# Row gathers of the last layer in bursts of 12, 8 and 12 instead of four bursts of 8

## The chip, the cores and the metric

The kernel runs on one core of a Trainium2 chip. The metric is the device time of one execution in microseconds (us), from runs of the whole program; lower is better. The rows and sums further down come from one profiled execution of the kernel before.

## What is computed

Four message-passing layers on a graph of 8192 nodes (32 features each) and 262144 edges sorted by destination. Each layer adds its result to x and normalises the rows:

```python
edge_index = jnp.stack([src, dst])
x = _layernorm(x + _L0_gnn_ref(x, L0_gnn_weight, src, dst, edge_type_64), axis=-1)
x = _layernorm(x + _L1_gnn_ref(x, edge_index, edge_weight), axis=-1)
x = _layernorm(x + _L2_gnn_ref(x, edge_index), axis=-1)
x = _layernorm(x + _L3_gnn_ref(x, edge_index, edge_attr_4, edge_attr_32, W1, b1, W2, b2, si_w0, si_w1), axis=-1)
```

The change touches the last layer, `_L3_gnn_ref`. For each edge a small network turns 32 edge features into 256 weights, and the message is made of these weights, of the source node's row (8 scalars s and 8 vectors v) and of 4 numbers sh of the edge:

```python
h = jax.nn.relu(edge_feat @ W1 + b1)
w = (h @ W2 + b2).reshape(e, 4, MUL, MUL)
s_e = s[src]
v_e = v[src]
m0 = ALPHA * (einsum('ei,eio->eo', s_e * sh0[:, None], w_000) + C110 * einsum('eim,em,eio->eo', v_e, sh1, w_110))
m1 = ALPHA * (einsum('ei,em,eio->eom', s_e, sh1, w_011) + einsum('eim,eio->eom', v_e * sh0[:, None, None], w_101))
out0 = jax.ops.segment_sum(m0, dst, num_segments=n)
out1 = jax.ops.segment_sum(m1.reshape(e, MUL * 3), dst, num_segments=n)
```

`s[src]` and `v[src]` are a gather of one row of 32 floats per edge.

## The kernel before

The edges are cut into 128 chunks of 2048. A chunk is 16 tiles of 128 edges, and 4 tiles are a group, so a chunk has 4 groups. The last layer holds four chunks at a time in the slots s = 0 to 3 of the buffer `gathered`; chunk c uses slot c mod 4. A pass of a loop over `it` handles four chunks, 32 passes (ROUNDS) in all.

For each chunk of the last layer the engines do this:

- **SP** (`stage(3)`, from L505): waits until the slot is free (`slot_freed`), then loads the 2048 source indices (`idx`, L512), the edge features (L515) and sh (L518).
- **POOL** (`gather_chunk`, L619 to L629): waits for the indices (L622) and issues 16 indirect DMAs (L626). Each fetches 128 rows of x by 128 indices, and tells of its landing on the semaphore of its group, `group_in[s][j // GROUP]`. Before some of the 16 it calls `pace(j)`, which for the last layer is `rests_3` (L668 to L674): where j is in RESTS_3, `rows_landed` (L662 to L666) makes POOL wait until the last group issued so far has landed. The first four chunks are gathered without any pacing (L694), the other 124 in the loop at L696.
- **PE** (`chunk3`): transposes the next chunk's edge features (L1285), makes its hidden units (L1296), multiplies out the weights of its groups (L1305), and sums the messages of the chunk before into destination windows with one-hot matrices (L1074).
- **ACT** (`chunk3`): copies and relu of the edge network (L904, L910), `scale_rows` of each group, which scales gathered rows by sh0 (L920, waits for `group_in`), and the one-hot matrices (L776, L789).
- **DVE** (`messages`, L1929 to L1980): 11 operations for each group; the first, `cprod` (L1940), waits for `group_in` as well and stands once per group. Then `add_chunk` (L1657 to L1669) and `release`, which frees the slot for SP.

So POOL can be up to four chunks ahead of DVE, and it is DVE's release that lets it into a slot. At the end of the layer ACT and DVE normalise most blocks beside the last chunks (L943 to L973, L2007 to L2021) and the last 8 blocks after the last chunk.

What sets the rests before the change:

```python
RESTS_3 = (0, 8)
...
if j in RESTS_3:
    rows_landed(s, j)
```

Of the kernel before, what the change touches and what calls it, by code (L numbers as in the profile page):

```python
# [9 lines left out]
SLOTS = 4  # L10
# [22 lines left out]
AHEAD = 12  # L33
MARKS_0 = [{8}, {2, 27}, {20}, {2, 27}, {20}, {13}, {0, 21}, {8, 30}]
MARKS_LATE = 2
RESTS_3 = (0, 8)
LEAD_0, LEAD_LATE = 6, 6
AHEAD_HI = 2
AHEAD_PARTS = 5
# [31 lines left out]
def build(nc, x, src, dst, edge_attr_32, edge_attr_4, edge_type_64, edge_weight, L0_gnn_weight,  # L71
# [15 lines left out]
    SET_LIST = [(n, m) for n in range(len(PARTS)) for m in range(2 if n < AHEAD_PARTS else 0, CHUNKS // WIDE)]  # L87
    SETS = len(SET_LIST)
    LOAD_SETS = [i for i, (n, _) in enumerate(SET_LIST) for _ in range(PARTS[n][1] // 4)]
    AHEAD_STEPS, AHEAD_STD = 6 * (ROUNDS - AHEAD), 2 * (ROUNDS - AHEAD)  # L90
    assert EARLY == TRIO * ROUNDS and LATE % SLOTS == 0 and WIDE * STRIP_D == SUPER * P
# [3 lines left out]
    with ExitStack() as ctx:  # L95
# [145 lines left out]
        rest = arena[:, 4096 * LOADS + 512:4096 * LOADS + 512 + BLOCKS * F].rearrange("p (b f) -> p b f", f=F)  # L241
# [183 lines left out]
        def is_dense(eng):  # L425

            eng.wait_ge(dense_known, 1)
            return numbers_at(eng, dense_ok[0:1, 0:1], 0, 1)[0]

        def is_regular(eng):  # L430

            eng.wait_ge(regular_known, 1)
            return numbers_at(eng, regular_ok[0:1, 0:1], 0, 1)[0]
# [27 lines left out]
        def looped(eng, first, end):  # L461

            return nc.Fori(first, end, engines=bass.OrderedEngineSet([eng.engine]), hint_back_edge=True)
# [136 lines left out]
        @block.gpsimd  # L600
        def _(pool):
            pool.iota(iota_i[:, :], [[1, P]], base=1, channel_multiplier=0).then_inc(iota_done, 1)
            pool.iota(part_i[:, :], [[1, 1]], base=0, channel_multiplier=1).then_inc(iota_done, 1)
            pool.iota(iota4_i.rearrange("p (c j) -> p c j", j=LANES), [[1, P], [0, LANES]], base=1,
                      channel_multiplier=0).then_inc(iota_done, 1)
            pool.iota(dst_of[:, :], [[P, BLOCKS + 2]], base=0, channel_multiplier=1).then_inc(iota_done, 1)

            pool.wait_ge(first_ready, 1)
            pool.wait_ge(records_out, 32)
            for b in range(BLOCKS):  # L610
                pool.indirect_dma_start(
                    csr[:, b, :, :].rearrange("p k w -> p (k w)"), None, records,
                    bass.IndirectOffsetOnAxis(ap=first_at[:, b:b + 1], axis=0)).then_inc(csr_in, 16)
            for k in range(4):
                pool.wait_ge(table_stored[k], 16 * (BLOCKS // TABLE_GROUP))
            due = [pool.alloc_register(f"idx_due_{s}") for s in range(SLOTS)]
            for s in range(SLOTS):
                pool.reg_mov(due[s], 16)
            def gather_chunk(l, s, pace=None):  # L619

                pool.wait_ge(idx_in[s], pool.snap(due[s]))
                pool.reg_add(due[s], due[s], 16)  # L622
                for j in range(TILES):
                    if pace is not None:
                        pace(j)
                    pool.indirect_dma_start(  # L626
                        gathered[:, s, j, :], None, rows[l],
                        bass.IndirectOffsetOnAxis(ap=idx[:, s, j:j + 1], axis=0),
                    ).then_inc(group_in[s][j // GROUP] if l == 3 else rows_in[l][s], 16)  # L629

            def gather(l):

                if l >= 1:
                    pool.wait_ge(rows_out[l - 1], 16)
                with looped(pool, 0, ROUNDS):
                    for s in range(SLOTS):
                        gather_chunk(l, s)

            regular = is_regular(pool)  # L640
            with pool.If(regular):
                mark = pool.alloc_register("mark_due")
                by_round = sum(len(marks) for marks in MARKS_0)

                def mark_passed():

                    pool.wait_ge(pe_mark, pool.snap(mark))
                    pool.reg_add(mark, mark, 1)

                def marks_0(j):  # L650

                    if j % (TRIO * TILES // by_round) == 0:
                        mark_passed()

                def marks_late(j):

                    if j % (TILES // MARKS_LATE) == 0:
                        mark_passed()

                landed = {(s, rest): pool.alloc_register(f"landed_{s}_{rest}") for s in range(SLOTS) for rest in RESTS_3}  # L660

                def rows_landed(s, rest):  # L662

                    last = (s - (rest == 0)) % SLOTS, (rest - 1) % TILES
                    pool.wait_ge(group_in[last[0]][last[1] // GROUP], pool.snap(landed[s, rest]))
                    pool.reg_add(landed[s, rest], landed[s, rest], 16 * GROUP)  # L666

                def rests_3(s):  # L668

                    def pace(j):  # L670

                        if j in RESTS_3:
                            rows_landed(s, j)
                    return pace  # L674

                pool.reg_mov(mark, by_round + 1 - LEAD_0)
                for s in range(TRIO):
                    gather_chunk(0, s)
                with looped(pool, 1, ROUNDS):
                    for s in range(TRIO):  # L680
                        gather_chunk(0, s, marks_0)
                pool.reg_mov(mark, ROUNDS * by_round + 1 - LEAD_LATE)
                with looped(pool, 0, LATE // SLOTS):
                    for s in range(SLOTS):
                        gather_chunk(0, s, marks_late)
                dense = is_dense(pool)
                with pool.If(dense < 1):
                    gather(1)
                    gather(2)
                for s in range(SLOTS):  # L690
                    for rest in RESTS_3:
                        pool.reg_mov(landed[s, rest], 16 * GROUP * (1 + (s > 0 or rest > 0)))
                pool.wait_ge(rows_out[2], 16)
                for s in range(SLOTS):  # L694
                    gather_chunk(3, s)
                with looped(pool, 1, ROUNDS):  # L696
                    for s in range(SLOTS):
                        gather_chunk(3, s, rests_3(s))
            with pool.Else():
                for l in range(4):  # L700
                    gather(l)
# [1369 lines left out]
```

## Time and profile before

| | us |
|---|---|
| median of 3 runs | 7251.59 |
| lowest and highest run | 7243.55, 7280.37 |
| profiled execution: its time | 7251.99 |
| profiled execution: span from the first to the last instruction | 7250.2 |
| PE busy in that span | 5598.4 (77%) |
| DVE busy | 4279.9 (59%) |
| POOL busy | 3945.7 (54%) |
| ACT busy | 2999.4 (41%) |

The last layer's gathers begin at 4127.8 us of the span and its messages at 4226.2 us, so it fills about the last 3000 us. In the rows of the profile, times are us from the start of the span, "x" counts instructions, and a bracket at the end of a timeline row gives how long the engine sat idle before the instruction and what ended that. "L626" is the line that issues the gathers. A busy POOL is here a POOL that writes the descriptors of a gather; the transfer itself runs on the DMA engines after that.

### The profile page before, as it was taken

The page shows a single profiled execution, that of the slowest core. Times are in us where ns is not written, and L with a number is a line of the kernel's source. Part 1 is how long each engine was busy: PE and PEld are TensorE (multiplying, and loading weights), DVE is VectorE, ACT ScalarE, POOL GpSimd, SP SyncE. Part 2 cuts the span into 40 slices and gives each one's busy share as a digit, 9 for nine tenths or more (in the row PEclk, how much of TensorE's full clock was granted, in tenths as well). Part 3 has the DMA queues.
Part 4 walks back from the last instruction along what each step waited for, and adds up shares of the span by engine and source line. Part 5 has one row for each costly group of instructions (what it writes and reads, how often), then busy time and mean ns, then how long its engine had stood idle before and what let it go on. Part 6 is the DMA issues. An engine that isn't in the chain of part 4 may idle for free.

```text
span 7250.2 us, 118009 instructions
## 1 busy us (share of the span) xinstructions
PE 5598.4 (77%) x38929; PEld 4300.2 (59%) x38930; DVE 4279.9 (59%) x8297; ACT 2999.4 (41%) x7294; POOL 3945.7 (54%) x4168
## 2 busy tenths in 40 slices
PE   7377777777777777666667668888888888888888
PEld 3177777676776766533333346666666666666666
DVE  4166656655556565311111058877887887888788
ACT  4244444444444444200000045555555555555556
POOL 1445555555555555555550146666666666666665
PEclk7587777777777778666667767777777777777777
DMA  9433333444444444687879601111111111111111
GB/s 318 145 150 145 141 136 130 165 162 149 171 151 163 150 162 163 211 283 269 277 242 296 199 15 25 24 23 24 24 24 23 24 24 23 24 24 24 23 25 24
DMA packets 596643, 865.44 MB, mean 119 GB/s; under 512 B 170833, under 2 KB 418706, under 8 KB 579474
## 3 DMA queue, kind: packets, MB, share of 16 engines
q1 hardware_dynamic: 363858, 385.79, 16.8%
q10 hardware_dynamic: 99520, 406.06, 14.2%
q0 software_dynamic: 133120, 71.57, 5.3%
q8 instruction: 102, 1.67, 0.1%
q14 instruction: 43, 0.35, 0.0%
HBM read 455.19 MB, written 406.85 MB: 119 GB/s over the span
## 4 chain that ended last, share of the span: by engine, by line
PE 37%; issue 24%; POOL 23%; another core or an unknown queue 5%; ACT 5%; DMA 3%; DVE 1%; ACTq 1%; POOLq 0%; SPq 0%; DVEq 0%
POOL gathered L626 23%; PE psum L1124 18%; PE psum L1074 9%; PE psum L1182 6%; ACT arena L806 3%; PE psum L1214 2%; DMA gathered<-x_rows,idx 1%; PE psum L1149 1%; ACT arena L805 1%; DMA arena<-counts 1%; PE psum L1016 1%; ACT table_out L724 1%; DMA arena<-adj 0%; DMA rel_table<-arena 0%
## 5 line engine op out<-in xcount | busy, mean ns | idle before, releaser
L626 POOL DMA_INDIRECT gathered<-rel_table,idx x2048 | 1933.6, 944 | 1676.6 <-issue 587.9
L626 POOL DMA_INDIRECT gathered<-x_rows,idx x2048 | 1949.3, 952 | 1443.3 <-issue 825.4
L1305 PE MATMUL psum<-w,arena 65*128 65x256 f32 x4096 | 1192.7, 443 | 214.2 <-DVE arena L1953 149.7
L805 ACT COPY arena<-psum 128x512 f32<-128x512 f32 x1024 | 603.4, 589 | 1562.0 <-PE psum L1124 1107.8
L1305 PEld LDWEIGHTS psum<-w,arena 65*128 65x128 f32 x4096 | 897.9, 227 | 394.2 <-DVE arena L1953 179.2
L1124 PE MATMUL psum<-arena 64*128 64x128 f32 x8192 | 699.7, 328 | 426.5 <-ACT arena L806 263.3
L1074 PEld LDWEIGHTS psum<-arena 128*128 128x128 f32 x4096 | 875.8, 244 | 220.6 <-issue 198.8
L1074 PE MATMUL psum<-arena 128*128 128x184 f32 x4096 | 953.0, 395 | 4.1 <-ACT arena L789 4.1
L1124 PE MATMUL psum<-table_out 64*128 64x128 f32 x8192 | 741.3, 347 | 242.9 <-ACT arena L806 183.9
L1124 PEld LDWEIGHTS psum<-arena 64*128 64x128 f32 x8192 | 637.9, 233 | 480.1 <-issue 258.3
L1124 PEld LDWEIGHTS psum<-table_out 64*128 64x128 f32 x8192 | 686.8, 253 | 288.1 <-ACT arena L805 181.7
L1953 DVE TENSOR_TENSOR arena<-psum,arena 128x256 f32<-128x256 f32 x1536 | 710.2, 490 | 190.4 <-ACT arena L920 153.6
L1074 PE MATMUL psum<-gathered,arena 128*128 128x32 f32 x4096 | 670.4, 327 | 98.8 <-issue 92.8
L910 ACT ACTIVATE arena<-psum,bias 65x512 f32<-65x512 f32 x512 | 324.9, 678 | 1013.7 <-PE psum L1296 644.4
L1074 PEld LDWEIGHTS psum<-gathered,arena 128*128 128x128 f32 x4096 | 653.6, 250 | 143.5 <-issue 136.1
L1296 PE MATMUL psum<-arena,w 32*65 32x512 f32 x1024 | 544.4, 997 | 172.2 <-ACT arena L910 107.1
L776 ACT ACTIVATE arena<-iota,key_all 128x128 f32<-128x128 f32 x2048 | 623.3, 390 | 0.0
L806 ACT CAST arena<-psum 128x512 fp8e4<-128x512 f32 x1024 | 612.1, 598 | 0.0
L1637 DVE TENSOR_TENSOR table_out<-iota,psum 128x2048 f32<-128x2048 f32 x128 | 292.8, 2288 | 485.7 <-PE psum L1124 244.2
L1637 DVE TENSOR_TENSOR arena<-iota,psum 128x2048 f32<-128x2048 f32 x128 | 292.8, 2287 | 476.3 <-PE psum L1124 288.7
L1182 PE MATMUL psum<-arena,xn 128*32 128x256 f32 x2976 | 395.1, 497 | 212.7 <-issue 195.5
L1669 DVE SCALAR_TENSOR_TENSOR acc<-psum,in_first,acc 128x32 f32 x128 | 32.0, 250 | 853.0 <-remote 428.2
(225 smaller groups left out, 5761.0 us busy)
## 6 DMA issues: line engine op xcount, KB each, us to landing
adj<-arena ACTq DMA_DIRECT2D x128, 2048.0 KB
arena<-adj SPq DMA_DIRECT2D x93, 2048.0 KB
counts<-arena ACTq DMA_DIRECT2D x128, 512.0 KB
arena<-counts SPq DMA_DIRECT2D x64, 1024.0 KB, 11.7
arena<-adj SPq DMA_DIRECT2D x40, 1024.0 KB
rel_table<-table_out ACTq DMA_DIRECT2D x32, 1024.0 KB
rel_table<-arena ACTq DMA_DIRECT2D x32, 1024.0 KB
gathered<-rel_table,idx POOLq DMA_INDIRECT x2048
```

Of the source, the lines that this page charges most:

```text
L626: pool.indirect_dma_start(gathered[:, s, j, :], None, rows[l], bass.IndirectOffsetOnAxis(ap=idx[:, s, j:j + 1], axis=0),).then_inc(group_i ...
L776: a = act.activation(onehot[:, s % 2, j, :], iota1[:, :], ACT.Square, scale=-1.0, bias=key_all[:, bass.ds(c * TILES + j, 1)])
L805: act.copy(w_to, made[:, 1]).then_inc(w_out, 1)
L806: act.copy(c_to, made[:, 0], saturate=False).then_inc(c_out, 1)
L910: act.activation(hidden[:, s % 2, q, :], bank_h[q % 2][0:HID + 1, :], ACT.Relu, bias=bias1[:, :]).then_inc(hidden_ready, 1)
L1074: mm = pe.matmul(bank[:, 0:message.shape[-1]], onehot_of(l, s)[:, j, :], message, start=(j == 0), stop=(j == TILES - 1))
L1124: mm = pe.matmul(psum[:, 2 * r + a, 2 * HIS * i:2 * HIS * (i + 1)], oh_lo[h][rows_of, u, :], oh_both[h][rows_of, u, :, :].rearrange("p k c ...
L1182: mm = pe.matmul(psum[F * g:F * g + F, bank_of(m), 4 * STRIP_D * (m % 2):4 * STRIP_D * (m % 2 + 1)] .rearrange("p (s d) -> p s d", d=STRIP_D),
L1296: pe.matmul(bank_h[q % 2][0:HID + 1, :], w1[F * q:F * q + F, :], edge_T[F * q:F * q + F, :], start=True, stop=True, tile_position=(F * q, ...
L1305: mm = pe.matmul(pair[g % 2][:, WN * q:WN * q + WN], hidden[:, s % 2, q, P * g:P * g + P], w2[:, :], start=True, stop=True)
L1637: dve.tensor_tensor(oh_lo[h], over(P), slot_of(0, P), ALU.is_equal).then_inc(half_ready, 1)
L1953: return dve.tensor_tensor(prod_v[:, :, m], split(w[:, :, Q_END:WN], MUL), over_o(zs[:, tiles, ZC + m:5 * MUL:3], MUL), ALU.mult)
```

## The change

RESTS_3 becomes one tuple for even and one for odd slots. Before, POOL waited before gather 0 and before gather 8 of every chunk, each time for the 8 gathers just issued. Now it waits in an even slot before gather 0 (for the last group of the chunk before) and before gather 12 (for group 2 of this chunk), and in an odd slot only before gather 4 (for group 0 of this chunk). Over two chunks the 32 gathers go out as 12, 8 and 12 with three waits instead of 8, 8, 8 and 8 with four. The registers that hold the awaited semaphore values are made and set for the new places. Nothing else changes.

```diff
-RESTS_3 = (0, 8)
+RESTS_3 = [(0, 12), (4,)]
...
-                landed = {(s, rest): pool.alloc_register(f"landed_{s}_{rest}") for s in range(SLOTS) for rest in RESTS_3}
+                landed = {(s, rest): pool.alloc_register(f"landed_{s}_{rest}") for s in range(SLOTS) for rest in RESTS_3[s % 2]}
...
-                        if j in RESTS_3:
+                        if j in RESTS_3[s % 2]:
                             rows_landed(s, j)
...
-                    for rest in RESTS_3:
+                    for rest in RESTS_3[s % 2]:
                         pool.reg_mov(landed[s, rest], 16 * GROUP * (1 + (s > 0 or rest > 0)))
```

POOL's instructions in the loop over 31 passes, slots 0 and 1, before the change (`group_in_0_1` is the semaphore of slot 0, group 1; `idx_in_1` that of slot 1's indices):

```order
L622 ISA [waits idx_in_0]
L666 REGISTER_ALU [waits group_in_3_3]
L626 DMA gathered<-x_rows,idx 128x32 x8
L666 REGISTER_ALU [waits group_in_0_1]
L626 DMA gathered<-x_rows,idx 128x32 x8
L622 ISA [waits idx_in_1]
L666 REGISTER_ALU [waits group_in_0_3]
L626 DMA gathered<-x_rows,idx 128x32 x8
L666 REGISTER_ALU [waits group_in_1_1]
L626 DMA gathered<-x_rows,idx 128x32 x8
```

The same place in the changed kernel:

```order
L622 ISA [waits idx_in_0]
L666 REGISTER_ALU [waits group_in_3_3]
L626 DMA gathered<-x_rows,idx 128x32 x12
L666 REGISTER_ALU [waits group_in_0_2]
L626 DMA gathered<-x_rows,idx 128x32 x4
L622 REGISTER_ALU [waits idx_in_1]
L626 DMA gathered<-x_rows,idx 128x32 x4
L666 REGISTER_ALU [waits group_in_1_0]
L626 DMA gathered<-x_rows,idx 128x32 x12
```

Four waits on `group_in` have become three, and the one at the border between slot 0 and slot 1 is gone: the burst of 8 runs across it, with only the wait for slot 1's indices inside. Slots 2 and 3 repeat the pattern, and no other engine's instructions move.

## Rows read from the trace of the kernel before

**Rows 1.** The page: busy tenths in 40 slices of the span.
```profile
PE   7377777777777777666667668888888888888888
...
POOL 1445555555555555555550146666666666666665
PEclk7587777777777778666667767777777777777777
```

**Rows 2.** Critical chain, 4333 to 7154 us: shares by line.
```profile
by line: POOL gathered L626 58.6%; issue 38.3%; DMA gathered<-x_rows,idx 2.4%; POOLq L666 0.3%; POOLq L622 0.3%; POOLq L696 0.1%; DMA idx<-in_src 0.1%; POOLq L621 0.0%; POOLq L665 0.0%; SPq L512 0.0%; DVEq L1987 0.0%
```

**Rows 3.** Line L626 by stretches: us, POOL busy (gathers), clock, DMA.
```profile
4263.70:5701.50 1437.80, 915.78 (x960) 0.75 0.11 24
5701.50:7135.10 1433.60, 912.25 (x960) 0.74 0.11 24
```

**Rows 4.** Line L1940, once per group, by stretches: us, DVE busy (count), clock.
```profile
4333.50:5087.10 753.60, 32.44 (x128) 0.74 0.11 24
5087.10:5830.50 743.40, 32.58 (x128) 0.75 0.11 24
5830.50:6489.10 658.60, 28.49 (x112) 0.74 0.11 24
6489.10:7154.00 664.90, 28.50 (x112) 0.74 0.11 24
```

**Rows 5.** Timeline: chunk 4's first gather and cprod, then chunk 124's.
```profile
4263.74 0.94 POOL L626 DMA_INDIRECT gathered<-x_rows,idx  x1 [55.59 <-DMA idx<-in_src]
...
4333.54 0.26 DVE L1940 TENSOR_TENSOR cprod<-gathered,sh 128x96 f32<-128x96 f32 x1 [0.43 <-issue]
...
7135.14 0.94 POOL L626 DMA_INDIRECT gathered<-x_rows,idx  x1 [2.11 <-issue]
...
7154.01 0.25 DVE L1940 TENSOR_TENSOR cprod<-gathered,sh 128x96 f32<-128x96 f32 x1
```

**Rows 6.** Waits, 4333 to 7154 us: total us, times, longest.
```profile
POOL gathered L626 <- DMA gathered<-x_rows,idx: 257.3, 122, 3.0
...
DVE arena L1953 <- ACT arena L920: 147.8, 75, 4.4
...
POOL gathered L626 <- DMA idx<-in_src: 2.7, 2, 2.4
...
ACT arena L920 <- DMA gathered<-x_rows,idx: 0.4, 1, 0.4
```

**Rows 7.** Waits, 7154 us to the end: total us, times, longest.
```profile
ACT arena L920 <- DMA gathered<-x_rows,idx: 7.1, 2, 3.6
```

**Rows 8.** Timeline of POOL around one rest (chunk 68).
```profile
5804.19 0.94 POOL L626 DMA_INDIRECT gathered<-x_rows,idx  x1 [0.30 <-issue]
5805.44 0.94 POOL L626 DMA_INDIRECT gathered<-x_rows,idx  x1 [0.30 <-issue]
5808.46 0.94 POOL L626 DMA_INDIRECT gathered<-x_rows,idx  x1 [2.07 <-DMA gathered<-x_rows,idx]
```

**Rows 9.** Timeline, the last chunk's end.
```profile
7225.35 0.26 DVE L1940 TENSOR_TENSOR cprod<-gathered,sh 128x96 f32<-128x96 f32 x1 [0.33 <-DMA gathered<-x_rows,idx]
...
7230.43 0.26 DVE L1940 TENSOR_TENSOR cprod<-gathered,sh 128x96 f32<-128x96 f32 x1 [0.22 <-issue]
...
7230.73 7.93 PE L1074 MATMUL psum<-arena 128*128 128x184 f32 x32 [4.07 <-ACT arena L789]
...
7231.55 0.49 DVE L1953 TENSOR_TENSOR arena<-psum,arena 128x256 f32<-128x256 f32 x1 [0.37 <-ACT arena L920]
...
7235.18 0.25 DVE L1978 TENSOR_TENSOR arena<-q_sum,sh 128x96 f32<-128x96 f32 x1
```

**Rows 10.** Line L626, the first chunks, gathered without rests: ns min/median/max, first and last start.
```profile
L626 POOL DMA_INDIRECT gathered<-x_rows,idx x63: 940/944/956, 4129.8 to 4207.2; - x63
```

**Rows 11.** Line L1940 without gathers beside it (first row) and with them.
```profile
L1940 DVE TENSOR_TENSOR cprod<-gathered,sh x5: 244/245/259, 4226.2 to 4261.3; 128x96 f32<-128x96 f32 x5
L1940 DVE TENSOR_TENSOR cprod<-gathered,sh x480: 237/255/323, 4333.5 to 7144.2; 128x96 f32<-128x96 f32 x160
```

## The prediction

> **What bounds the kernel now.** I began with the page's slices. The change lives in the last layer, slices 24 to 40, and there nobody is full: PE is at 8 tenths and POOL at 6, with PE's granted clock at 0.7 [rows 1]. So the layer is a loop with two runners: POOL, which gathers rows ahead, and the consumers (PE, ACT and DVE, chained group by group), which use them.
>
> The chain of work that ended last blames POOL. Of 4333 to 7154 us it puts 58.6% on the gathers and nearly all the rest on "issue", the pauses between them [rows 2]. This must be read with care: the chain starts at the very end, finds the last chunk waiting for its gather, and then walks back along POOL, which never waits for anybody. That POOL is busy without a break says that it has been behind its allowance; it does not say that anyone has waited for it. So I compared paces and distance.
>
> POOL takes 1437.8 us for 960 gathers, which are 60 chunks, or 23.96 a chunk, and then 1433.6 for the next 60, or 23.89; 23.93 on average [rows 3]. The consumers' pace comes from L1940, 4 a chunk: 753.6/32 = 23.55, 743.4/32 = 23.23, 658.6/28 = 23.52 and 664.9/28 = 23.75, together 2820.5/120 = 23.50 [rows 4]. They are 0.43 a chunk faster than POOL. The distance shows the same: chunk 4's first gather leads its use by 4333.54 - 4263.74 = 69.8 us, chunk 124's by 7154.01 - 7135.14 = 18.9 [rows 5]. 50.9 us are used up in 120 chunks, 0.42 each. **POOL is the slower runner, but starts with a lead that lasts almost to the end.** Up to chunk 124 the consumers waited for landed rows once, for 0.4 us in ACT's scaling; their real waits are for each other (DVE for ACT's scaling, 147.8 us) [rows 6]. After that ACT waits twice, 7.1 us in sum [rows 7]. So the rests cost the kernel almost nothing until its last chunk, and there is nothing left over either: a POOL slower than today would push the end back one for one.
>
> "Within 0.5%" below means 7215.3 to 7287.9 us, about what a measurement of this kernel can tell from no change.
>
> **The change part by part.**
>
> *One rest fewer per two chunks, on POOL.* Gathers in a burst start 1.25 us apart (5804.19, 5805.44), and idle before one is 0.30; behind a rest it is 2.07 [rows 8]. The 122 rests that the waits name add up to 257.3 us, 2.11 each [rows 6], so a rest costs 2.11 - 0.30 = 1.81. The loop handles 124 chunks: 62 rests go, 62 x 1.81 = 112 us of POOL's time, 0.91 a chunk. POOL's pace becomes 23.93 - 0.91 = 23.02, now faster than the consumers' 23.50. Per pair of chunks that leaves three rests.
>
> *Longer bursts.* Gathers 9 to 12 of a burst are new. 63 gathers in a row without a rest started between 4129.8 and 4207.2 us: 77.4/62 = 1.25 apart, and the longest took 956 ns [rows 10]. So I cost them at nothing on POOL. That was beside idle PE and DVE, so it bounds the price from below. No row shows the landing after more than 8. Lower bound 1.81 for a rest; upper bound the longest idle before a gather that waited for a landing, 3.0 - 0.30 = 2.7 [rows 6]. I take 1.81, since the awaited group is always the last 4 gathers and what it waits for is their landing alone.
>
> *What POOL gains with it.* It may be only as far ahead as slots are free. The lead stays at its start value of 60 to 70 us instead of shrinking, and POOL's spare 0.48 us a chunk goes into waits for `idx`, which today end only 2 of its waits for 2.7 us [rows 6]. SP's queue is not touched: the same three loads per release, at the same moment of DVE.
>
> *What the consumers gain.* Through chunk 124, the 0.4 us that ACT waited. In the last chunk ACT's two waits of 3.5 and 3.6 us go [rows 7]; the one-hot matrices come earlier, and the last matmuls need not start as late as 7230.73. But they also need DVE's messages. These ended at 7235.18 + 0.25 = 7235.4, of which DVE had lost 0.33, 0.22 and 0.37, together 0.9, to the last gathers and to ACT's scaling behind them. Today the matmul block of 16 tiles ends at 7230.73 + 7.93 = 7238.7 [rows 9]; afterwards it can end when the last group's 4 of 16 tiles (7.93/4 = 2.0) follow the messages: 7235.4 - 0.9 + 2.0 = 7236.5, 2.2 us earlier. Nothing behind it (fold, last 8 blocks, store) changes.
>
> Sum: 0.4 + 2.2 = 2.6, taken as 3 us. The profiled execution took 7251.99 (its span 7250.2 and 1.8 around it), 0.4 above the median of 7251.59, so I make no correction: 7251.99 - 3 = **7249 us**.
>
> *A rule that speaks against the change.* cprod (L1940) reads two operands in SBUF. With no gather beside it 5 of them took 244 to 259 ns, and 480 beside POOL's gathers had a median of 255 and a longest of 323 [rows 11]; not one was held for a gather's 944. 
>
> **The rivals.**
>
> 1. *The last quarter was braked.* The consumers ran at 23.75 in the last 28 chunks and at 2155.6/92 = 23.43 before [rows 4]. With the lead down to 18.9, POOL may have cut off their quick stretches without leaving a wait of note. Then 28 x 0.32 = 9 more come back: 7240. Against it: 0.4 us of waits, and stretches of 23.55 when the lead was large. 20%.
>
> 2. *The chain is right and POOL bounds throughout.* Then all of the 112 come back: 7251.99 - 112 = 7140. For it: 58.6% of the chain. Against it: a lead of 69.8 us, and 0.4 us of waits. 3%.
>
> 3. *Slower: the landing takes longer after longer bursts.* 12 gathers in flight instead of 8 queue up in the DMA rings, and each of the three rests grows. Four rests of 1.81 are 7.24 a pair; three equal them at 2.41 each. Up to there POOL is no slower than now; beyond it every 0.1 of a rest costs 62 x 3 x 0.1 = 19 us, because the last chunk has no slack today. At the 2.7 of the longest idle this is 8.1 - 7.24 = 0.86 a pair, 62 x 0.86 = 53: 7305. Against it: the even pitch over 63 gathers, and a DMA share of 0.11 [rows 4]. 5%.
>
> 4. *Slower: DVE needs the rests*, the lock. If the consumers lost what the rests lose, 0.91 a chunk, they would take 120 x 0.91 = 109 longer: 7361. 2%.
>
> 5. *Nothing changes*, because in an execution where the consumers are slow all the way (one run took 7280.37) the gathers end no wait at all. That is inside the forecast's range.
>
> **How the numbers follow.** The forecast (the consumers keep their own pace, only the end moves) gets 70%. Its range is the scatter of that pace: the quickest stretch, 23.23, held for 120 chunks gives 120 x 0.27 = 32 less, 7217; the slowest, 23.75, gives 30 more, 7279. Rival 1's 7240 lies inside, rivals 2, 3 and 4 outside, with tails of both likely cases: near 1.5 in 10 left out. Faster by over 0.5%: rival 2, and the low tails of forecast and rival 1, 5% and 4%: 0.12. Slower: rivals 3 (half of it) and 4, and a high tail of 4%: 0.08. Within 0.5%: 0.80.
>
> **What would show it.** In the changed kernel's profile POOL has three long idles per 32 gathers (186 in the loop instead of 248), each near 2.1; bursts stay at a pitch of 1.25. Chunk 124's first gather leads its L1940 by about 60 to 70 us instead of 18.9. POOL's waits ended by `idx` rise from 2 to many, some 60 us in sum. ACT's L920 waits for no gather in the last chunk. The chain leaves POOL for PE, ACT and DVE. The consumers' pace stays within 23.2 to 23.8. Wrong would be: a lead that still shrinks, rests of 2.4 or more, L1940 or other DVE operations clearly longer, or a consumers' pace well below 23.2, which would mean that the rests or the lead reached into their pace by a way I do not see.

## The result and the profile after

| | before | changed |
|---|---|---|
| median, us | 7247.57 (4 runs) | 7942.0 (4 runs) |
| lowest to highest | 7242.22 to 7280.37 | 7914.21 to 7961.48 |
| profiled execution, us | 7251.99 | 7961.48 |
| its span | 7250.2 | 7959.7 |

The changed kernel took **1.095 times the time of the one before, interval 1.0908 to 1.0993**: 9.5% slower. The range of the forecast ended at 7279.

**The same kernel has two kinds of times here, whatever the version.** In the runs above and in three of the five sets that follow (a set is some kernels timed together, with the kernel before among them) the kernel before took 7250 us (once 7402); in the other two it took 6153. I call the first kind the **slow setting** and the second the **quick setting**. What sets them apart from outside is not known; the last section comes back to it. The result above belongs to the slow setting, and so do [rows 1 to 11].

The page of the changed kernel, slices of the span, answers to [rows 1]:

```profile
PE   6477777777777776666666777777777777777777
...
POOL 2355555555555555555114555555455555555553
PEclk7577787778777776676786666666666666667667
```

From slice 24 on PE is down from 8 tenths to 7, POOL from 6 to 5, the granted clock from 0.7 to mostly 0.6. All engines got emptier, so somebody waits. The chain of work that ended last, 4350 to 7860 us, answers to [rows 2] (the view itself cuts the row off):

```profile
by line: another core or an unknown queue 19.4%; PE psum L1305 18.1%; issue 15.8%; PE psum L1296 13.9%; PE psum L1074 7.3%; DVE arena L1961 3.9%; DVE arena L1953 3.8%; ACT arena L920 3.7%; ACT arena L776 3.3%; DVE arena L1975 3.0%; ACT aren
```

POOL has left the chain, as forecast. What has come in is "another core or an unknown queue" with 19.4%. There is only one core. The view says this when a wait has ended and it finds nobody whose work had ended just before.

The stretches of L1940 (us, DVE busy, count, clock), one start for each group, answer to [rows 4]:

```profile
4354.20:5287.50 933.30, 32.47 (x129) 0.69 0.09 19
5287.50:6227.90 940.40, 32.50 (x129) 0.69 0.09 19
6227.90:7049.00 821.10, 28.78 (x114) 0.69 0.09 20
7049.00:7860.00 811.00, 28.07 (x111) 0.70 0.09 20
```

From the first cprod of chunk 4 to that of chunk 124 it is 3505.8/120 = **29.2 us a chunk, in place of 23.50**. 120 x 5.7 = 684 of the 709 us lost are here. It is there from the first stretch on, while POOL's lead stays near 80 us, so no gather is late.

PE also got slower: over these 120 chunks it was busy 2680.3 us, 22.3 a chunk at a granted clock of 0.69, where the kernel before took 2452.7 us for them, 20.4 a chunk at 0.74. DVE's 19.1 a chunk stayed. So some of the 5.7, at most 1.9, may be slower matmuls that follow from the idling and not the waiting itself; no run separates the two.

The waits, 4354 to 7860 us (total, times, longest), answer to [rows 6]:

```profile
ACT arena L904 <- remote: 1052.6, 120, 10.2
POOL gathered L626 <- DMA idx<-in_src: 911.0, 121, 10.2
...
DVE arena L1946 <- remote: 459.1, 92, 9.8
DVE arena L1946 <- PE psum L1305: 271.9, 72, 7.6
POOL gathered L626 <- DMA gathered<-x_rows,idx: 168.1, 80, 2.2
...
ACT arena L789 <- remote: 52.7, 20, 4.4
```

and for the kernel before, 4333 to 7154 us, rows of the same answer as [rows 6] that I had not used:

```profile
DVE arena L1946 <- remote: 186.2, 80, 4.6
ACT arena L904 <- remote: 128.4, 37, 7.2
...
ACT arena L789 <- remote: 3.3, 2, 1.6
```

POOL now waits for free slots (`idx`, 911 us): its part of the forecast came true. But DVE at L1946 waits for PE's weights, ACT at L904 for PE's transposes, and ACT at L789 for its own squares (L776), all ended by "remote". L789 is the clearest, since both ends are one engine. The timeline of the changed kernel around one burst of 12, which starts at 5903.31:

```profile
5903.31 0.94 POOL L626 DMA_INDIRECT gathered<-x_rows,idx  x1 [8.19 <-DMA idx<-in_src]
...
5909.98 1.95 PE L1305 MATMUL psum<-w,arena 65*128 65x256 f32 x8
...
5911.48 2.43 ACT L776 ACTIVATE arena<-iota,key_all 128x128 f32<-128x128 f32 x8
...
5917.03 0.94 POOL L626 DMA_INDIRECT gathered<-x_rows,idx  x1 [0.30 <-issue]
...
5918.24 2.00 ACT L789 ACTIVATE arena<-arena,one_col 128x2048 f32<-128x2048 f32 x1 [4.34 <-remote]
...
5920.08 0.94 POOL L626 DMA_INDIRECT gathered<-x_rows,idx  x1 [2.11 <-DMA gathered<-x_rows,idx]
...
5920.26 0.42 DVE L1946 TENSOR_TENSOR arena<-psum,gathered 128x256 f32<-128x256 f32 x1 [7.76 <-remote]
```

ACT's squares end at 5913.9 and its own next instruction starts 4.34 us later. PE's weights were there at 5911.93; DVE, free since 5912.5, sees them at 5920.26, beside the end of the burst. The work is done and **the signal of it arrives late**: the trace records the semaphore updates at 5918.14 (ACT's) and 5920.23 (PE's).

To measure this I took from each trace the 512 pairs of PE's last L1305 of a group and DVE's L1946, and kept those before which DVE had sat idle (over 0.2 us), from the loop's first gather on. They are called idle L1946 below. An undisturbed signal takes 0.04 us. In the kernel before, 14 signals sent within the first three gathers of a burst all took 0.04 us, 10 within the fourth 2.33 us on average, 21 within the fifth 3.20. Of the 117 that were late by over 0.8 us there, 97 arrived 11.0 to 12.0 us after the burst's first gather, whenever they had been sent; the burst's last gather ends 9.7 us after it.

Not every signal is late. The trace records many of the semaphore updates themselves. In the two stretches of the waits above, of the recorded updates that belong to one engine, PE's came over 0.5 us behind the instruction's end in 111 of 198 (before) and 240 of 240 (changed), ACT's in 34 of 452 and 120 of 428, and DVE's in 0 of 2502 and 0 of 3511.

One number ties this to the gathers. Rows of the kernel before, from its waits of 4127 to 4219 us, when 64 gathers go out without a rest [rows 10] and PE, ACT and DVE do the small self products beside them:

```profile
DVE acc L1923 <- remote: 84.1, 5, 24.2
ACT group_xT L898 <- remote: 82.8, 6, 24.4
```

These products stood still 24 us at a time, and the last stop ended at 4218.3, 90.5 us after the first gather's start: 90.5/64 = 1.41 us a gather, while POOL issues one per 1.25. And 8 x 1.42 = 11.4, the place where the late signals of a burst of 8 arrive. **Theory A** came from that: each gather leaves about 1.42 us of work on something that signals of PE and ACT need too; POOL issues faster than that; a rest lets it catch up. What that something is stays a supposition throughout.

### The profile page after: what moved, and what is told of

Same layout as the page of the kernel before. It is cut to its first block, busy times and chain, and to the rows that moved or that the text cites. A ratio compares the mean times of both kernels' runs of the same rounds, so it can differ in the third digit from the quotient of the medians.

```text
span 7959.7 us, 117945 instructions
## 1 busy us (share of the span) xinstructions
PE 5836.0 (73%) x38929; PEld 4371.9 (55%) x38930; DVE 4284.9 (54%) x8297; ACT 3002.6 (38%) x7294; POOL 3935.2 (49%) x4168
## 4 chain that ended last, share of the span: by engine, by line
PE 52%; issue 16%; another core or an unknown queue 13%; ACT 9%; DVE 8%; DMA 2%; ACTq 1%; DVEq 0%; SPq 0%
PE psum L1124 17%; PE psum L1074 11%; PE psum L1305 8%; PE psum L1296 6%; PE psum L1182 5%; ACT arena L806 2%; DVE arena L1961 2%; DVE arena L1953 2%; ACT arena L920 2%; ACT arena L776 2%; PE psum L1214 1%; DVE arena L1975 1%; DMA arena<-counts 1%; PE psum L1149 1%
## 5 line engine op out<-in xcount | busy, mean ns | idle before, releaser
L626 POOL DMA_INDIRECT gathered<-x_rows,idx x2048 | 1938.5, 947 | 2102.6 <-DMA idx<-in_src 981.9
L626 POOL DMA_INDIRECT gathered<-rel_table,idx x2048 | 1934.0, 944 | 1677.7 <-PE psum L1124 625.9
L1305 PE MATMUL psum<-w,arena 65*128 65x256 f32 x4096 | 1364.7, 485 | 451.3 <-DVE arena L1953 335.6
L1305 PEld LDWEIGHTS psum<-w,arena 65*128 65x128 f32 x4096 | 970.2, 246 | 747.7 <-DVE arena L1953 395.7
L1074 PEld LDWEIGHTS psum<-arena 128*128 128x128 f32 x4096 | 853.0, 238 | 223.4 <-issue 204.2
L1074 PE MATMUL psum<-arena 128*128 128x184 f32 x4096 | 932.0, 388 | 6.5 <-DVE arena L1978 3.3
L1296 PE MATMUL psum<-arena,w 32*65 32x512 f32 x1024 | 580.6, 1082 | 227.7 <-ACT arena L904 123.9
L1946 DVE TENSOR_TENSOR arena<-psum,gathered 128x256 f32<-128x256 f32 x512 | 215.6, 421 | 848.9 <-remote 473.5
L776 ACT ACTIVATE arena<-iota,key_all 128x128 f32<-128x128 f32 x2048 | 623.3, 390 | 0.0
## 6 DMA issues: line engine op xcount, KB each, us to landing
arena<-counts SPq DMA_DIRECT2D x64, 1024.0 KB, 11.3
```

Of the source, the lines that this page charges most:

```text
L626: pool.indirect_dma_start(gathered[:, s, j, :], None, rows[l], bass.IndirectOffsetOnAxis(ap=idx[:, s, j:j + 1], axis=0),).then_inc(group_i ...
L776: a = act.activation(onehot[:, s % 2, j, :], iota1[:, :], ACT.Square, scale=-1.0, bias=key_all[:, bass.ds(c * TILES + j, 1)])
L1074: mm = pe.matmul(bank[:, 0:message.shape[-1]], onehot_of(l, s)[:, j, :], message, start=(j == 0), stop=(j == TILES - 1))
L1296: pe.matmul(bank_h[q % 2][0:HID + 1, :], w1[F * q:F * q + F, :], edge_T[F * q:F * q + F, :], start=True, stop=True, tile_position=(F * q, ...
L1305: mm = pe.matmul(pair[g % 2][:, WN * q:WN * q + WN], hidden[:, s % 2, q, P * g:P * g + P], w2[:, :], start=True, stop=True)
```

## The experiments

Against theory A stood rival B (the change is slow in itself, by the missing rest or POOL's faster pace, not by the length of bursts). Each edit is against the kernel before, and the change to the awaited value only follows the place of the rest.

**Bursts of 12 and 4, and of 10 and 6**, with two rests a chunk as before.

```diff
-RESTS_3 = (0, 8)
+RESTS_3 = (0, 12)
```

(and `(0, 10)`). Expected of 12 and 4:

> Bursts of 12 and 4 gathers in every chunk: as many rests as before (two a chunk), so POOL's pace should stay near 23.9 us a chunk. Theory A (backlog): each gather leaves about 1.42 us of work on some path that PE's and ACT's semaphore signals share, POOL issues one per 1.25 us, and a signal is held until the backlog is empty. 12 gathers need 17.0 us, the next burst starts after 12 x 1.25 + 1.83 = 16.8, so the backlog runs into the burst of 4 and empties only after 16 x 1.42 = 22.7 us of 23.6: slow, 7600 to 7950 us. Theory B (lead): what slows the consumers is that POOL is now as far ahead as the slots allow and waits for free slots: here the pace is the old one, so 7250 us, within 30.

Expected of 10 and 6:

> Bursts of 10 and 6, again two rests a chunk. Theory A: 10 gathers need 14.2 us, the next burst starts after 14.3, so the backlog just empties in each rest; signals are held until 14.2 instead of 11.4 us after the start of the long burst, and 8.5 of the short one: 7250 to 7400 us, clearly below the 12 and 4 kernel. Theory B: 7250 us, equal to it.

**Short rests**, each for the group before the last one:

```diff
-                    last = (s - (rest == 0)) % SLOTS, (rest - 1) % TILES
+                    last = (s - (rest == 0)) % SLOTS, (rest - 1 - GROUP) % TILES
```

> Four rests per two chunks and bursts of 8 as before, but each waits for the group before the last, which has landed already or nearly, so a rest lasts 0 to 0.7 us instead of 1.8. Theory A: 8 gathers need 11.4 us and get 10 to 10.7: the backlog never empties until POOL waits for a slot: as slow as the change or slower, 7900 us or more. Theory C (length of the burst alone, so that any wait after 8 resets it): 7250 us. Theory B expects slow as well.

**Rests in the first four chunks too:**

```diff
+                def first_rests(s):
+                    def pace(j):
+                        if j == 8:
+                            pool.wait_ge(group_in[s][1], 16 * GROUP)
+                        if j == 0 and s > 0:
+                            pool.wait_ge(group_in[s - 1][3], 16 * GROUP)
+                    return pace
...
-                    gather_chunk(3, s)
+                    gather_chunk(3, s, first_rests(s))
```

> The kernel before, with the same rests (before gathers 0 and 8) in the layer's first four chunks too, whose 64 gathers went out without any. Theory A: in the kernel before PE's signals to ACT and DVE in the self products arrived up to 24 us late while those 64 gathers ran, and the layer's first message operation started at 4226 us; with rests it starts 60 to 80 us earlier, and everything behind it shifts: 7170 to 7200 us. Theory B: nothing changes, 7250 us, or 13 us more for seven rests.

Measured: this set met the quick setting, and every number above was for the slow one. Before 6153.83 (25 runs); 12 and 4: 6150.52, ratio 0.9991 (0.9981 to 1.0002); 10 and 6: 6150.82, 0.9994 (0.9984 to 1.0004); short rests: 5702.23, **0.9264** (0.9246 to 0.9283); first rests: 6161.74, 1.0015 (1.0005 to 1.0024). The waits of 12 and 4, 3205 to 6046 us:

```profile
ACT arena L920 <- DMA gathered<-x_rows,idx: 768.9, 224, 6.7
...
POOL gathered L626 <- DMA gathered<-x_rows,idx: 516.3, 238, 2.5
...
DVE arena L1946 <- PE psum L1305: 67.8, 106, 1.2
```

No "remote" is left, and none of 91 idle L1946 was late. The consumers wait for gathers (L920): POOL is the bound, at its 23.9 a chunk. As predictions of a time all four missed. What follows: late signals belong to a setting, and without them rests are pure loss (short rests).

**The change again, bursts of 4, no rests, short rests again**, in one set:

```diff
-RESTS_3 = (0, 8)
+RESTS_3 = (0, 4, 8, 12)
```

and `RESTS_3 = ()` for no rests.

> The changed kernel itself, a second time, beside the kernel before on the same chip, because the kernel before has by now taken 7248 us in one set of runs and 6154 in another, and the change was only timed in the first set. Theory A (signals of PE and ACT are held up behind a train of gathers, about 1.42 us for each gather where POOL issues one per 1.25; this is there in the 7248 set and absent in the 6154 set): where the kernel before takes about 7248, 7942 as before; where it takes about 6154, POOL is the bound there (23.9 us a chunk), the change gives back 0.91 a chunk, 124 x 0.91 = 112: 6042, with ACT's L789 starting 0.1 us behind its squares throughout. Rival B (the change is slow by itself, whatever the set): ratio 1.095 in both, 6738 where the kernel before takes 6154.

> Bursts of 4 in the loop, a rest behind each (four rests a chunk in place of two). POOL's own pace becomes 16 x 1.25 + 4 x 1.85 = 27.4 us a chunk. Theory A: where the kernel before takes about 7248, a burst of 4 is over long before a backlog builds up (4 x 0.17 = 0.7 us against a rest of 1.85), so late signals vanish (DVE's L1946 'remote' waits near 0), and POOL's pace alone sets the time: first gather 4137 + 80 + 120 x 27.4 + 112 for the end = 7617, which is faster than the changed kernel's 7942 with more rests. Where the kernel before takes about 6154: 6154 + 124 x 3.5 = 6590, no late signals. Rival B' (what costs time is the number of waits for landings or gathers in flight as such, not the length of an unbroken train): late signals stay as in the kernel before, 1.5 to 2 us a chunk, and the time is above 7700 on the 7248 kind.

> No rests in the loop; only the free slots hold POOL back. Theory A: on the 7248 kind each gather adds 0.17 us of backlog with nothing to drain it but the waits for a free slot; consumers get slower until POOL waits for them at every chunk: pace at least the 29.2 us a chunk of the changed kernel, so 7940 or more, and late signals of up to 24 us as in the first 64 gathers. On the 6154 kind: POOL at 20.0 a chunk is no bound any more, consumers run at their own 20.1 (DVE full): 5700, within 30. Rival B (length of bursts costs on any chip): above 6154 on the 6154 kind.

> Rests at 0 and 8 that wait for the landing of the group before the last one. It took 5702 us where the kernel before took 6154. Theory A: on the 7248 kind the rest is so short (0.3 us more than an ordinary gap) that the train of gathers is practically unbroken, so it should lose there what the changed kernel loses or more: 7900 or above; on the 6154 kind again 5702. Rival C (the two sets differ only in something before the last layer, and gathers hold nobody up): ratio 0.93 on both kinds, 6740 where the kernel before takes 7248.

Measured, slow setting, before 7255.73 (7 runs): the change 7911.18, 1.0918 (1.0876 to 1.0959); bursts of 4 7659.23, 1.0565 (1.0528 to 1.0602); no rests 8245.88, 1.1366 (1.1327 to 1.1404); short rests 8220.65, **1.1337** (1.1296 to 1.1378). The kernel that won 7.4% in one setting loses 13.4% in the other. Its waits here, 4330 to 8110 us:

```profile
POOL gathered L626 <- DMA idx<-in_src: 1388.5, 120, 14.0
...
DVE arena L1946 <- remote: 800.1, 142, 11.3
...
ACT arena L789 <- remote: 272.5, 78, 5.0
```

and those of the bursts of 4, 4300 to 7560 us:

```profile
ACT arena L920 <- DMA gathered<-x_rows,idx: 1165.8, 344, 6.7
POOL gathered L626 <- DMA gathered<-x_rows,idx: 1014.9, 475, 3.3
...
DVE arena L1946 <- PE psum L1305: 1.6, 3, 1.2
```

With twice as many rests none of the idle L1946 is late, of which there are only 4; of the updates recorded in 4300 to 7528 us 18 of 184 from PE came over 0.5 us late, at most 1.75, and none of 461 from ACT. Only POOL's own pace is left (27.5 us a chunk; expected were 27.4 and a time of 7617). PE's granted clock was 0.71 in this stretch, below the 0.74 of the kernel before, so it is not a lower clock that makes signals late. It is faster than the change, with more than twice its rests. Rival B' (waits as such cost) falls with this, and rival C, that nothing in the last layer differs, with the short rests.

**10 and 6, 12 and 4 again, and an even spread.** The spread replaces full rests by waits of 0.57 us for the group that ended two gathers ago:

```diff
-RESTS_3 = (0, 8)
+RESTS_3 = [{1: 2, 5: 2, 9: 2, 13: 2}, {1: 2, 5: 2, 9: 2, 12: 1}]
...
-                    last = (s - (rest == 0)) % SLOTS, (rest - 1) % TILES
+                    lag = RESTS_3[s % 2][rest]
+                    last = (s - (rest < lag)) % SLOTS, (rest - lag) % TILES
```

The fourth kernel does this in the first four chunks as well.

> Bursts of 10 and 6: as many rests as before (two a chunk), only the lengths differ, so POOL's own pace stays 23.9. It took the time of the kernel before where that was 6154. Theory A (a train of gathers leaves 1.42 us each on a path that signals of PE and ACT share, and it is issued at 1.25): on the kind where before takes about 7250 what counts is how far into a burst a signal falls. With late signals from the fifth gather on, (b - 4)^2 summed a chunk: 32 for 8/8, 72 for 12/8/12 (per chunk), 40 for 10/6; consumers lose 3.4 us a chunk at 32 and about 9 at 72, so about 4.3 at 40: 24.4 a chunk, 7355. On the 6154 kind: same as before. Rival (number of rests counts, not their place): 7250 or 6154, same as before.

> Bursts of 12 and 4, with as many rests as before. Theory A: 64 on the same scale, so some 7 us a chunk over the unhindered 20.1: 27 a chunk, 7680 where before takes about 7250; same as before where that takes 6154. Rival (it is the missing rest, POOL's faster pace, that costs in the changed kernel): same as before on both. This run and the one with 10 and 6 change only lengths, never the number of rests.

> The loop's gathers spread evenly: at j = 1, 5, 9 and 13 a wait for the landing of the group that ended two gathers earlier, which by the measured 3.07 us behind a full rest delays the next start by 3.07 - 2 x 1.25 = 0.57 us; in odd slots the one at 13 is replaced by a full rest at 12. Per two chunks 40 + 7 x 0.57 + 1.83 = 45.8 us, 22.9 a chunk, against 16 x 1.42 = 22.7 of work on the shared path: a backlog never gets longer than a few gathers. Theory A: no late signals in the loop, POOL at 22.9 is the bound on both kinds: first gather about 4110 + 80 + 120 x 22.9 + 112 = 7050 where before takes about 7250 (0.972), 3086 + 80 + 2748 + 112 = 6026 where it takes 6154 (0.979). Rival (any unbroken stretch above 4 gathers, or a gather rate above 16 in 23.9 us, costs the consumers): slower than before where before takes 7250, since here no rest but one in two chunks is a full one.

> The same spreading in the first four chunks too, ahead of the loop. Theory A: on the 7250 kind the 64 gathers in a row that hold up the self products for 24 us at a time go (L898 and L1275 run through in about 25 us instead of 102), the first chunks' consumers start some 70 us earlier, but POOL bounds the rest at 22.9 a chunk: 4110 + 92 + 2748 + 112 = 7062, within 0.5% of the one before. On the 6154 kind 6038.

Measured, slow setting, before 7256.56 (7 runs): 10 and 6 7484.29, 1.0323 (1.0295 to 1.0351); 12 and 4 **8013.29**, 1.1045 (1.0998 to 1.1092); even 7596.57, 1.0465 (1.0437 to 1.0493); even from the start 7615.67, 1.0492 (1.0463 to 1.052). The waits of 12 and 4, 4336 to 7932 us, against the quick ones above:

```profile
ACT arena L904 <- remote: 808.7, 120, 9.9
...
DVE arena L1946 <- remote: 541.2, 115, 8.3
...
ACT arena L789 <- remote: 204.9, 71, 4.3
```

Here the number of rests is that of the kernel before, and the loss is a little larger than the change's. So it is the length of the bursts and not the rest that was taken away. The sizes were off (expected 7355 and 7680): longer bursts cost more than my (b - 4) squared. In the kernel with 10 and 6 all 27 signals to an idle L1946 that were sent within the first four gathers of a burst of 6 were late, by 4 to 7 us on average, although a full rest had just ended; in the kernel before, 14 of 14 at the first three places were on time. So what the burst before has left over counts too.

The even spread missed by 547 us, on the wrong side of 1. Its POOL did what was asked (next starts 1.83 us behind the short waits, in place of 1.25), yet 180 of 206 idle L1946 were late, those sent from the ninth to the thirteenth gather behind a full rest (69 of 78 late) by 4.5 to 7.9 us on average. A first-in-first-out path with 1.42 us a gather does not do that. It is what the rival in the forecast named: more than 16 gathers in 23.9 us cost the consumers. Together with the 97 of 117 signals that came just when the whole burst was worked off, it suggested **theory A2**: a signal that meets more than a short backlog waits until the path is *empty*. A load of nearly 100% then holds signals for long even if the backlog stays short, and slack inside the burst should help much.

**A short wait inside each burst of 8; bursts of 5, 5 and 6; first rests again.**

```diff
-RESTS_3 = (0, 8)
+RESTS_3 = {0: 1, 5: 2, 8: 1, 13: 2}
...
-                    last = (s - (rest == 0)) % SLOTS, (rest - 1) % TILES
+                    last = (s - (rest == 0)) % SLOTS, (rest - RESTS_3[rest]) % TILES
```

and `RESTS_3 = (0, 5, 10)`.

> As the kernel before (full rests at 0 and 8), and in the middle of each burst of 8 a short wait, at 5 and 13, for the landing of the group that ended two gathers earlier: it delays the next start by 0.57 to 0.61 us, so 8 gathers are issued in 10.0 + 0.6 us, and 2 x 0.6 = 1.2 us a chunk are added to POOL's 23.9: 25.1. Theory A2 (late signals wait until the shared path is empty, at 1.42 us a gather, and only those sent when some 0.7 us or more of backlog are queued are held): at gather 5 the backlog of 4 x 0.17 = 0.7 us is worked off by the 0.6, so late signals fall from the 119 of the kernel before to below 40; POOL bounds: 4110 + 80 + 120 x 25.1 + 112 = 7314 where before takes 7256. Theory A1 (first in, first out behind the gathers of a burst, by its length): as many late signals as in the kernel before and a time of 7350 or more. On the 6154 kind both: 6154 + 124 x 1.2 = 6303.

> Full rests at 0, 5 and 10: bursts of 5, 5 and 6, three rests a chunk; between the two rests of the kernel before (8 and 8) and the four of the run with bursts of 4. In the kernel before signals sent behind up to 3 gathers of a burst were on time and those from the fourth on 2 to 4 us late. Theory A, both forms: late signals are few and short (below 40 of more than 0.5 us, none above 4 us), consumers could do less than 24 a chunk, POOL bounds at 20.0 + 3 x 1.83 = 25.5: 4110 + 80 + 3060 + 112 = 7362. Rival (there is a cost for each rest to the consumers): above 7362. On the 6154 kind 6154 + 124 x 1.8 = 6377.

> The kernel before with its rests in the first four chunks too. It cost 8 us where before takes 6154. Where before takes 7256: theory A: the 64 gathers in a row there hold up the self products for 24 us at a time; with rests L898 and L1275 run through in 25 to 40 us instead of 102, the consumers start the loop 60 us earlier, so the lead of 65 us at chunk 4 is about 5 and they wait for POOL from the start; POOL's own end moves back by 7 x 1.83 = 13 us: 7256 + 13 - (up to 5) = 7265, same within 0.5%. Were the consumers the bound, as my forecast had it for the changed kernel, the 60 us would come off: 7196.

Measured, before 7401.8 in this set (19 runs): short wait inside 7474.17, 1.0097 (1.0062 to 1.0132; expected 7314/7256 = 1.008); 5, 5, 6: 7577.18, 1.0236 (1.0181 to 1.0292; expected 1.015); first rests 7364.53, 0.995 (0.9915 to 0.9985). Waits of the kernel with the short wait inside, 4379 to 7343 us:

```profile
ACT arena L920 <- DMA gathered<-x_rows,idx: 802.2, 283, 6.8
...
ACT arena L904 <- remote: 21.6, 7, 6.4
...
DVE arena L1946 <- remote: 11.3, 6, 3.7
```

With 0.6 us of air in the middle of a burst L1946's "remote" is 11.3 us, against 186.2 in the kernel before and 227.9 in the kernel with first rests of this same set, which has full bursts of 8 in the loop (144 of its 158 idle L1946 were late). POOL becomes the bound. That is theory A2's forecast (under 40 late; 15), and not that of A1, where bursts of 8 stay as bad. But the short waits also slow POOL from 23.9 to 25.2 us a chunk, and no run has the break without the lower rate: which of the two removed the late signals is open.

The first rests gained 37 us where I expected no change. The lead went from 66 us at chunk 4 to 59 at chunk 124, so the consumers' 24.22 a chunk was the bound; and their first L1940 of chunk 4 came 176 us behind the layer's first gather, against 206 in the kernel before's trace. That fits a gain from the earlier start; the kernel before of this set has no trace to compare.

**The change and no rests once more:**

> The changed kernel once more, in the hope of the kind of chip where the kernel before takes 6154. There: POOL is the bound at 23.9 a chunk, one rest fewer per two chunks gives back 0.91 a chunk, 124 x 0.91 = 112: 6042, ratio 0.982. Where before takes 7250 again 1.092 to 1.095; where it takes 7400 the changed kernel, limited by late signals and hardly by POOL, some 8000, ratio 1.08.

> No rests in the loop. Where the kernel before takes 6154: 5700 within 30 (POOL 20.0 a chunk, DVE nearly full); where it takes 7250: 8246 again, 1.137; where it takes 7400: 8250 to 8400.

Measured, quick setting, before 6152.33 (7 runs): **the change 6025.65, ratio 0.9797 (0.9781 to 0.9814), faster by 2%**; no rests 5695.62, 0.9256 (0.9241 to 0.9271). Waits of the change here, 3200 to 5900 us:

```profile
ACT arena L920 <- DMA gathered<-x_rows,idx: 676.0, 238, 6.4
...
POOL gathered L626 <- DMA gathered<-x_rows,idx: 383.0, 177, 2.9
...
DVE arena L1946 <- PE psum L1305: 33.1, 52, 1.2
```

The main runs on one page (pace: consumers' us a chunk, chunks 4 to 124; late: signals over 0.5 us from PE to an idle DVE, with the sum of their delays; DVE was idle for only part of it, 261 of the 375 us before and 814 of the 1239 in the changed kernel):

| kernel | setting | pace | late of idle | late in all, us | median, us |
|---|---|---|---|---|---|
| before, 8/8 | slow | 23.50 | 119 of 153 | 375 | 7248 |
| changed, 12/8/12 | slow | 29.2 | 174 of 191 | 1239 | 7942 |
| 10/6 | slow | 25.48 | 184 of 199 | 822 | 7484 |
| 12/4 | slow | 29.97 | 230 of 236 | 1643 | 8013 |
| even spread | slow | 26.66 | 180 of 206 | 936 | 7597 |
| no rests | slow | 31.50 | 175 of 180 | 1502 | 8246 |
| short rests | slow | 31.47 | 197 of 201 | 1650 | 8221 |
| 8/8, first rests | slow | 24.22 | 144 of 158 | 537 | 7365 (before 7402) |
| short wait inside 8/8 | slow | 24.70 | 15 of 53 | 44 | 7474 (before 7402) |
| 5/5/6 | slow | 25.37 | 5 of 13 | 8 | 7577 (before 7402) |
| 4/4/4/4 | slow | 27.05 | 0 of 4 | 0 | 7659 |
| 12/4 | quick | 23.68 | 0 of 91 | 0 | 6151 |
| changed, 12/8/12 | quick | 22.69 | 0 of 52 | 0 | 6026 |
| no rests | quick | 20.08 | 0 of 30 | 0 | 5696 |
| short rests | quick | 20.04 | 0 of 33 | 0 | 5702 |

At the same number of rests, two a chunk, late signals and time rise with the length of the longer burst (8, 10, 12). No version beats both kernels in both settings. In the slow one the first rests were 0.5% better than the kernel before (in the set at 7402 alone), in the quick one no rests are 7.4% better.

## Why the prediction was wrong

*What failed is one step: "Longer bursts. ... So I cost them at nothing on POOL. That was beside idle PE and DVE, so it bounds the price from below."* For POOL the price of nothing is right: the pitch within bursts of 12 is still 1.25. But I asked only what longer bursts cost the engine that issues them. Their price is paid by the consumers: PE's and ACT's signals arrive late, and the consumers' pace went from 23.50 to 29.2, 5.7 us a chunk or 684 us. And the sentence on idle engines was false in a telling way. PE, ACT and DVE were not idle beside those 63 gathers; they were stuck. The self products took from 4123.1 to 4225.3 us. In the quick setting the same instructions (L1275) ran from 3081.4 to 3105.3. I had quoted the gathers' side of that stretch as [rows 10] and not looked at the "remote" of 24 us beside it.

*"The consumers keep their own pace" (23.50)* fell with it. 23.50 was not their own pace but one with 290 us of idling before L1946 in 120 chunks. Unhindered they ran at 20.08 in the quick setting (no rests). If their own pace is the same in the slow one, which no run shows, they gave up some 3.4 us a chunk in the kernel before already. I had read the waits of [rows 6] for gathers, and "their real waits are for each other" covered a "remote" of 186.2 us that names nobody.

*What POOL gains* was right: lead near 80 us, no shrinking, POOL's waits ended by `idx`, POOL gone from the chain. *One rest fewer* was right too: in the quick setting POOL's pace was 23.91 with two rests a chunk (12 and 4) and 22.90 in the changed kernel, 1.01 less (forecast 0.91), and 124 x 1.01 = 125 of the 127 us gained there (6152.33 - 6025.65).

*Rival 2* (POOL bounds throughout, 112 us back) had 3%. In the slow setting it is wrong, in the quick one it is what happens.

*Rival 3* (the landing takes longer) is not what made it slower: the idle before a gather that waited for a landing was 168.1/80 = 2.10 us on average and at most 2.2, against 2.11 and 3.0 [rows 6], and the last packet of a gather landed 1.04 us behind its end as before. *Rival 4* (DVE held by the lock) had the right sign and the wrong mechanism. DVE's operations did not get longer. From the groups by line, changed kernel, 4300 to 7800 us:

```profile
L1953 DVE TENSOR_TENSOR arena<-psum,arena 128x256 f32<-128x256 f32 x1440 | 663.9, 489 | 213.0 <-ACT arena L920 160.5 <-issue 52.5
...
L1940 DVE TENSOR_TENSOR cprod<-gathered,sh 128x96 f32<-128x96 f32 x480 | 121.5, 253 | 34.6 <-issue 34.1
```

489 and 253 ns, against 490 and 254 before. The rule of a port lock between DVE and GpSimd in the Trainium skill, "SBUF — State Buffer", section "Who interferes with whom", would have a DVE instruction with two SBUF inputs blocked while a GpSimd instruction reads SBUF. Neither trace shows that: L1940 is neither longer nor kept waiting (34.6 us of idle before 480 of them, 34.3 in the kernel before), so it explains nothing of the 9.5%.

The prediction's list of what would show me wrong did name the case ("the rests or the lead reached into their pace by a way I do not see"), but no rival stood for it. Longer trains of the operation that all else is paced around, with "remote" waits in the trace, should have had far more.

## What to carry to other kernels

A wait that the profile puts down to "remote" or to an unknown queue in a program on one core can be a late signal, as it was here: take the producer's end and the consumer's start, and see what the difference goes with. If an engine issues a long train of indirect gathers, look at what the *other* engines do beside the longest train that is already in the trace; in the slow setting a short pause in the middle of 8 came with nearly no late signals, and 12 in a row cost a quarter of the pace. And time a pacing change in more than one session with the kernel before beside it, since here its sign depended on the setting.

## What the runs showed of the hardware

- Signals of PE and ACT (PE to DVE, ACT to itself) normally took 0.04 to 0.12 us. In the slow setting behind four or more unbroken indirect gathers from POOL they mostly took 2 to 12 us, and up to 24 behind 64. Each gather counted for 1.41 to 1.42 us, POOL issued one per 1.25. DVE's recorded updates were never late (0 of 3511 in the changed kernel).
- When a held signal gets through is not settled. What is shared is not shown by any row. If each gather takes 1.42 us in turn, 103 of the 119 late signals in the kernel before (all over 0.5 us) arrived within 0.7 us of the moment when nothing was left, as theory A2 has it, but only 51 of 174 in the changed kernel and 65 of 180 in the even spread; most of the others came earlier. In the order of issue (theory A) it is 35, 4 and 29. So neither form describes the changed kernel, and that long trains bring late signals stands on the runs, not on a theory of the path.
- In the quick setting none of this was seen, not even without any rest (0 late of 30). The gathers themselves looked alike in both: 1.25 us apart, landed 1.0 to 1.2 us behind their end. The first three layers also end 1000 to 1100 us earlier there (the last layer's gathers begin at 3076 to 3086 us, not 4083 to 4205), and they too show "remote" waits of up to 26.9 us in the slow setting.
- What makes the setting is open. The runs named chips by number: quick on 3 and 6, slow on 4, 15 and again 6 (whether that was the same piece of silicon is not known). So it is not simply a property of a chip. No kernel here changes the setting, and none was made to test for its cause.
